# Squares of the feature parts moved from ScalarE to GpSimd in an eight-batch mixture-attention kernel

## The reference, cut to what matters

```python
q = jnp.einsum('bnsd,neod->bneso', sx, wq)
k = jnp.einsum('bnsd,nod->bnso', sx, wk)
v = jnp.einsum('bnsd,nod->bnso', sx, wv)
scores = jnp.einsum('bnesd,bntd->bnest', q, k) * d ** 0.5 + causal
att = jax.nn.softmax(scores, axis=-1)
qkv = jnp.einsum('bnest,bntd->bnesd', att, v)
```

## Time and profile before

| | us |
|---|---|
| median of 3 runs | 1468.18 |
| lowest and highest | 1465.44, 1469.33 |
| profiled execution, its time | 1463.23 |
| profiled execution, its span | 1461.5 |
| TensorE busy | 1208.4 |
| VectorE busy | 887.3 |
| ScalarE busy | 844.6 |
| GpSimd busy | 268.3 |

### The profile page before, as it was taken

The page is one execution under the profiler, slowest core; times in us unless marked ns, Lnnn a source line. Parts: engine busy times, 40 slices in busy tenths (PEclk is TensorE's granted clock), DMA queues, the critical chain, the costliest instruction groups (busy, mean ns, idle before and its releaser), DMA issues.

```text
span 1461.5 us, 29125 instructions
## 1 busy us (share of the span) xinstructions
PE 1208.4 (83%) x11006; PEld 611.2 (42%) x11103; DVE 887.3 (61%) x2048; ACT 844.6 (58%) x1057; POOL 268.3 (18%) x569
## 2 busy tenths in 40 slices
PE   4896548890579989999998999999999999999963
PEld 3453347670235434433443443344334344334421
DVE  4825873339664654685566568557565845855445
ACT  0231124451565777587667757867776875777750
POOL 2000050004011122121212211211221221222210
PEclk9997869996579999999999999999999999999985
DMA  8989279902392048008304801830560291075000
GB/s 151 203 156 214 27 148 203 197 1 49 92 140 27 14 88 119 2 13 154 60 14 96 118 1 38 143 48 13 113 102 2 70 130 29 13 133 73 2 17 10
DMA packets 121007, 117.72 MB, mean 81 GB/s; under 512 B 73452, under 2 KB 90107, under 8 KB 120713
## 3 DMA queue, kind: packets, MB, share of 16 engines
q1 hardware_dynamic: 116820, 115.31, 43.7%
q10 hardware_dynamic: 3733, 0.60, 0.3%
q0 software_dynamic: 320, 0.04, 0.0%
HBM read 88.07 MB, written 22.95 MB: 76 GB/s over the span
## 4 chain that ended last, share of the span: by engine, by line
PE 37%; DVE 11%; issue 8%; ACT 8%; DMA 5%; SPq 3%; POOL 2%; POOLq 0%; DVEq 0%; ACTq 0%
PE b_pso L1984 13%; PE b_pss L1960 10%; ACT b_pb L2110 6%; PE b_psm L2011 3%; DMA qk_parts_b<-b_qs 3%; DMA b_qop<-bound_part 3%; PE b_psm L2041 2%; PE b_psm L2027 2%; POOL b_pb L2150 2%; PE b_psm L1943 1%; PE b_psm L2020 1%; DVE b_rq L2233 1%; SPq L1895 1%; PE b_psm L2023 1%; SPq L1894 1%
## 5 line engine op out<-in xcount | busy, mean ns | idle before, releaser
L2110 ACT ACTIVATE b_pb<-b_pss 128x1024 f32<-128x1024 f32 (+2 forms) x736 | 659.7, 934 | 261.3 <-PE b_pss L1960 181.0
L1984 PE MATMUL b_pso<-b_pb,b_vop 128*32 128x77 f32 (+4 forms) x5376 | 374.7, 385 | 19.5 <-POOL b_pb L2150 15.2
L2150 POOL TENSOR_SCALAR_AFFINE_SELECT b_pb<-b_pb 128x256 f32<-128x256 f32 (+1 forms) x544 | 221.7, 424 | 821.2 <-ACT b_pb L2110 816.2
L1960 PE MATMUL b_pss<-b_qop,b_kop 128*128 128x512 bf16 (+3 forms) x1439 | 318.6, 327 | 31.3 <-DMA b_qop<-bound_part 10.9
L1960 PEld LDWEIGHTS b_pss<-b_qop,b_kop 128*128 128x128 bf16 x1536 | 124.0, 100 | 209.8 <-ACT b_pb L2110 98.2
L1984 PEld LDWEIGHTS b_pso<-b_pb,b_vop 128*32 128x32 f32 x5376 | 112.6, 109 | 194.1 <-issue 167.1
L2318 DVE TENSOR_TENSOR b_ofm<-b_pso,b_mk 128x512 f32<-128x512 f32 (+1 forms) x96 | 51.7, 538 | 136.5 <-PE b_pso L1984 135.5
L918 PE MATMUL psc<-tz,ub 128*64 128x128 f32 x1152 | 80.2, 284 | 45.0 <-DVE tz L1030 36.2
L2011 PEld LDWEIGHTS b_psm<-w_mixer,b_ofm 128*128 128x128 f32 (+1 forms) x576 | 68.8, 186 | 64.3 <-DVE b_ofm L2318 31.8
L918 PEld LDWEIGHTS psc<-tz,ub 128*64 128x64 f32 x1152 | 71.9, 141 | 53.2 <-DVE ub L1026 33.9
L2194 DVE COPY b_ot<-b_psm 128x336 f32<-128x336 f32 (+1 forms) x96 | 39.9, 416 | 82.6 <-PE b_psm L2011 81.0
(11 more groups left out here) (420 smaller groups left out, 1511.9 us busy)
## 6 DMA issues: line engine op xcount, KB each, us to landing
b_qop<-qk_parts_b SPq DMA_DIRECT2D x192, 144.0 KB
tz<-taps SPq DMA_DIRECT2D x64, 304.0 KB, 9.5
x<-in_x SPq DMA_DIRECT2D x16, 1024.0 KB, 13.4
qk_parts_b<-b_qs SPq DMA_DIRECT2D x16, 864.0 KB, 5.1
b_kop<-qk_parts_b SPq DMA_DIRECT2D x192, 36.0 KB
b_mk<-b_mskf SPq DMA_DIRECT2D x128, 36.0 KB, 4.9
qk_parts_b<-b_ks SPq DMA_DIRECT2D x8, 432.0 KB, 4.0
n_late<-id_d SPq DMA_DIRECT2D x1, 2400.0 KB, 9.6
```

The source lines that it names most:

```text
L1960: mm = pe.matmul(pss[:, u % 2, b, col:col + w], lhs, qop[:, n, e, q0:q0 + w], start=True, stop=True, skip_group_check=True)
L1984: mm = pe.matmul(pso[VW * ee:VW * (ee + 1), (3 * n + x) % 2, q0 - QT * x:q0 - QT * x + w], vop[0:r, j, n, :], pb[0:r, slot_, b, cc:cc + w] ...
L2110: nc.scalar.activation(pb[:, s % PB, 0:nb, 0:w], pss[:, s % 2, 0:nb, 0:w], ACT.Exp, scale=float(HD) ** 0.5).then_inc(exped, 1)
L2150: ins = pool.affine_select(out=v_, in_=v_, compare_op=ALU.is_ge, fill=0.0, base=0, pattern=pat, channel_multiplier=-1)
```

## The change

In `split` on ScalarE the square and its waits go. GpSimd gets a function `square` that multiplies the first part by itself, after the mask of the same step. Nothing else differs; the squares' six slots, the order of the jobs and the readers of `squares` are as they were.

```diff
                     if i == 0:
                         act.wait_ge(spilled, (p + 1) * 48 + 16)
-                    if i >= 6:
-                        act.wait_ge(free, base + at + 1)
                     nc.scalar.copy(dst, psm[0:m, (parity(p) + at) % 2, 0:FB]).then_inc(part0, 1)
-                    act.wait_ge(part0, (p + 1) * 9 + i + 1)
-                    nc.scalar.activation(squares[0:m, slot[c], :], dst, ACT.Square).then_inc(squared, 1)
...
+                def square(p, base, at, c):
+
+                    g, x = c
+                    i = FEATS.index(c)
+                    m = P if g < 2 else D
+                    src = qs[:, 0, g, x * FB:(x + 1) * FB] if g < 2 else ks[:, 0, x * FB:(x + 1) * FB]
+                    pool.wait_ge(part0, (p + 1) * 9 + i + 1)
+                    if i >= 6 or p >= 0:
+                        pool.wait_ge(free, base + at + 1)
+                    pool.tensor_tensor(squares[0:m, slot[c], :], src, src, ALU.mult).then_inc(squared, 1)
+                    pool.wait_ge(squared, (p + 1) * 9 + i + 1)
+
                 def run(p, att, pro, prev):
+                    at = jobs(att, pro, prev)
+                    n_jobs = 0
                     for s in range(SPAN):
                         if att:
                             mask(p, s)
+                        for kind, c in at.get(s, ()):
+                            if kind == "feat":
+                                square(p, jobs_before(p), n_jobs, c)
+                            n_jobs += 1
```

## The result

The changed kernel takes 1484.62 us in the median (1483.54 to 1490.66, 4 runs), beside 1466.81 for the kernel before (1463.3 to 1469.33, 4 runs). The ratio is 1.0132, 95% interval 1.0096 to 1.0167: 14 to 24 us slower, 1.0132 being 19.4 us. Forecast were 1484.9 us and 16.7 us more.

The account below looks back on a forecast made before the run. The period was taken to be set by when the last feature's parts are ready, through spill and load. VectorE held by squares: 15.0 us over seven periods plus 1.7 ahead of the attention, +16.7 on 1468.18, giving 1484.9 us; range 1463 to 1500.

Parts of the forecast that it names:

- The relief: ScalarE without squares: TensorE's waits of 0.58 and 0.17 us go, at most 0.75 us a period; fast-side bound 27 us.
- The multiply: Each new GpSimd multiply of 384 elements a partition takes 0.92 us, at 2.15 ns an element plus some 0.1 us.
- Waits for squares and masks: The change's new waits cost nothing: squares fit before later masks and end before their readers need them.
- The hold: VectorE stands still while GpSimd runs, stretched by GpSimd's end minus VectorE's start, less 0.15 us; up to 0.77 each.
- Features (2,0) and (2,1): Early in a period, their squares stretch VectorE's cast and the row behind it, all on the path: +0.69 and +0.75 us.
- From (1,0) to (1,1): Mid-period, squares hold VectorE: +0.8 us for (1,0) and (0,1), +0.35 for (1,1); half taken, 0.58.
- (1,2): Last feature of a period: its square delays VectorE's cast directly ahead of the spill, +0.20 us.
- Ahead of the attention: Batch 0's features, where VectorE sets the pace: 0.2 to 0.4 us for each of five features, +1.7 us.
- The sum: 2.2 us a period, 15.0 over seven periods with the first losing less, plus 1.7 ahead of the attention: +16.7 us.
- The signs: Profile after: cast and third-step medians 0.2 to 0.6 us higher, b_ofm wait 2 us, spill 2 us later.
- ScalarE's relief winning: Rival: squares fall in VectorE's slack and TensorE's waits go, 5.3 us less, 1463 us; chance 0.12.
- everything falls on the path: Rival: 63 stretches of 0.77 us, 48.5 us more, 1517, or masks late too; over 1497 us, chance 0.10.

Follow-up runs that it names:

- relief: Changed kernel without any squares: the tile is filled with ones once and ScalarE only counts; ratio 0.9981 to the kernel before, 2.8 us less.
- half: Changed kernel with GpSimd multiplying 192 of the 384 columns, the other half of the squares left out; ratio 1.0030 to the kernel before, 4.4 us more.
- both: Kernel before, ScalarE keeping its squares, plus the change's GpSimd multiplies into a tile that nobody reads; ratio 1.0135 to the kernel before.
- write_only: Kernel before, ScalarE keeping its squares, plus GpSimd fills that read nothing at the multiplies' places; ratio 1.0067 to the kernel before, 9.8 us more.
- ahead_only: Changed kernel with all nine squares on GpSimd ahead of the attention and all others on ScalarE; ratio 1.0022 to the kernel before, 3.2 us more.
- three_beside: Changed kernel with only (2,2), (0,0) and (0,2) squared on GpSimd beside the attention, all others on ScalarE; ratio 0.9971 to the kernel before.
- five_beside: Beside the attention GpSimd squares (2,2), (0,0), (0,2) and, after step 54's exponential, (2,0), (2,1); ScalarE the rest; ratio 0.9996 to the kernel before.
- other_seven: Changed kernel with the squares of (2,0) and (2,1) back on ScalarE, the other seven on GpSimd; ratio 1.0056 to the kernel before, 8.2 us more.
- first_two: Changed kernel with only the squares of (2,0) and (2,1) on GpSimd, the other seven on ScalarE; ratio 1.0094 to the kernel before, 13.8 us more.
- held_back: Changed kernel with (2,0) and (2,1) multiplied later beside the attention, behind step 54's exponential; ratio 1.0029 to the kernel before, 4.3 us more.

## Why the prediction was right

- **What bounds the kernel.** The chain through the last feature's parts, the spill and the loads held: the spill moved by 3.0 us in the third period (107.4 to 110.4), the period by 2.9 (126.0 to 128.9), and the wait for the DMA hardly.
- **The relief**, at most 0.75 us a period. `relief` gives 2.8 us for eight batches, 0.4 a period, in an interval that reaches past nothing; the spill of the fourth period moved by 0.8. The caution that VectorE must let it through was right: its 0.60 stayed. The bound of 27 us is excluded.
- **The multiply.** Taken at 0.92 us from the 4608-element row; measured 0.82. By `half` it is 1.6 ns an element and 0.2 us fixed, where I had 2.15 ns and 0.1 us: two errors that nearly cancel.
- **Waits for squares and masks**, costed at nothing: `both` shows it, since it has the loss with no one waiting for the multiply. TensorE's waits for masks even shrank. Ahead of the attention it did wait for squares, 1.6 to 1.8 us three times in place of 1.2; but that stretch is 24.4 us long in `both` too, where those waits are 1.2 as before.
- **The hold**, (GpSimd's end - VectorE's start) - 0.15. At the two places shown it gives 0.53 and 0.62 and the profile has 0.54 and 0.62, and all 45 casts keep to it within 15 ns. What I had not told apart, and `write_only` did, is that instructions with two SBUF inputs are held only by work that reads.
- **Features (2,0) and (2,1)**, 0.69 + 0.75 = 1.44 us: measured 1.16. Both terms carried the multiply's 0.1 too much.
- **From (1,0) to (1,1)**, 0.58 us as half of 1.15 (the fourth and fifth entry of the list, which the prediction calls the third and fifth). TensorE's waits there add up to 2.22 us (0.25, 0.30, 0.54, 0.64 and 0.49) against 1.57 before (0.58, 0.22, 0.60, 0.17): 0.65. The sizes agree, though not the places: I had the feature matmul wait longer, and it was two output products. Nor do the holds: the cast of (1,0) took 0.25 us more where I had 0.4, L2293 (now L2307) 0.03 where I had 0.6, and the mixing step beside (1,1) 0.65 where I had 0.52. That half of the sum came out is luck.
- **(1,2)**, 0.20 us directly ahead of the spill: its cast took 0.40 in place of 0.36 us, so 0.04.
- **Ahead of the attention**, +1.7 us: `ahead_only` gives 3.2 (0.6 to 6.0), and the stretch in the profile after is 2.4 us longer with VectorE busy 2.3 more. With all nine multiplies there it is 24.4 us in `both` and ahead_only, with none 21.7 in `relief`, three_beside and five_beside. So the term was 0.7 us or more too low.
- **The sum.** Without the falls of the clock the fourth period has the spill at 109.0, 1.7 us later than before (107.3), where I had 2.2: a period's terms were too high by a quarter, 12 us in seven periods in place of 15. But in the profile the spills of the seven periods are 19.0 us later in all. Falls of the clock, which the prediction didn't have, make most of the difference: 1.5 us each behind `b_ofm` in three periods, and about 1 us each at the start of two. The first period is also 2.7 us later at its spill, and in it the clock was at 0.50 for 6.8 us from 448.9 on, which it was not before. So the total came out closer than the working deserves.
- **The signs.** I had said that the medians of cast and third step rise by 0.2 to 0.6 us. The cast's rose by 0.04 and the third step's by 0.16, and the latter beside masks. The wait for `b_ofm` (1.81 for 2) and the later spill were as said.
- **Rivals.** ScalarE's relief winning is excluded by `both` and `relief`. That everything falls on the path, 48.5 us, is excluded by the loss of 19.4 itself, and by other_seven: seven squares cost 8.2 us, 1.2 each, against 6.9 each for the first two.

## What to carry to other kernels

GpSimd's idle share says nothing about what work on it costs: ask which VectorE instructions run beside it, whether they have two SBUF inputs or run in a fast mode, and whether anybody waits for the chain that they are in. A relieved engine is worth only what the next in line lets through; here VectorE stood behind ScalarE with 0.60 us of its own. If such work has to go to GpSimd, put it where VectorE has just handed over its result: the nine multiplies cost 10 to 15 us less with two of them two to four steps later.

## What the runs showed of the hardware

- TensorE's granted clock fell to 0.50 for 3.4 us directly behind a wait of 1.81 us for `b_ofm`, in three of the six periods that have this wait in the changed kernel, and in two of six each in `both` and first_two; behind the same wait at 0.65 (before, held_back, other_seven), at 1.06 (half) and at 1.17 (write_only) it never did. A fall moved the next spill by 1.5 us. So a stall that is longer by 1.16 us can cost 2.7. The counts are of one profiled execution of each kernel, and falls stand at other places too: at starts of periods behind the DMA, and in the first period behind a wait of 1.06 us in seven of the thirteen profiles, while the other six have the same wait and no fall.
- A fill of GpSimd leaves VectorE's instructions with two SBUF inputs alone and holds the cast; a multiply holds both, by the time that it still has to run less 0.15 us. A step with one input in PSUM was not held (558 ns). VectorE holds GpSimd in the same way: a multiply took up to 1.39 us in place of 0.82.
- The multiply of two bf16 inputs takes 0.82 us for 384 elements and 0.52 for 192: 1.6 ns an element and 0.2 us fixed.
- One of the two 864 KB transfers of the `qs` spill, the second, takes 5.6 us in most periods and up to 7.6 in others of the same execution; in the kernel before it is 5.59 to 7.33 us. What it meets was not tried.
